# Attention written out as straight code, with a later transposition of the maxima and the sums behind the products with V

## What is computed

```
scores = einsum('bhqd,bhkd->bhqk', q, k) / sqrt(32)      # 16 heads of 32
scores = where(causal, -inf, scores)                     # self attention only
attn   = softmax(scores, axis=-1)
out    = einsum('bhqk,bhkd->bhqd', attn, v)
```

## Time and profile before

| | us |
|---|---|
| median of 3 runs | 4899.39 (4897.51 to 4901.42) |
| the profiled execution | 4905.71 |
| its span | 4904.1 |

### The profile page before, as it was taken

How to read it: one execution, slowest core, us unless ns; L and a number is a source line. 1 busy time by engine, 2 the same in 40 slices (tenths; PEclk the granted TensorE clock), 3 DMA queues, 4 the chain that set the end, 5 groups by cost and what they waited for, 6 DMA issues and landing times. The chain is left out here.

```text
span 4904.1 us, 74698 instructions
## 1 busy us (share of the span) xinstructions
PE 4388.1 (89%) x23024; PEld 2724.6 (56%) x23024; DVE 3038.8 (62%) x5530; ACT 2192.0 (45%) x4027; POOL 2321.7 (47%) x790
## 2 busy tenths in 40 slices
PE   7988999997889979999999999999996649898998
PEld 5864555546668854444444444444443427686776
DVE  4436776753633347777777777777772546676776
ACT  1213555551221105666656565556563115544554
POOL 0012333330000017888988888888894123433445
PEclk8987999998889978999999999999998869999999
DMA  4554443406455560222322222222202552322232
GB/s 143 183 164 104 105 106 89 91 16 233 169 178 175 176 159 4 53 58 58 67 53 63 53 63 57 55 53 55 53 6 99 195 181 89 97 95 92 94 108 99
DMA packets 328345, 488.99 MB, mean 100 GB/s; under 512 B 22440, under 2 KB 188328, under 8 KB 321832
## 3 DMA queue, kind: packets, MB, share of 16 engines
q1 hardware_dynamic: 318472, 468.01, 34.3%
q10 hardware_dynamic: 7232, 8.40, 0.6%
q0 software_dynamic: 2304, 8.39, 0.5%
HBM read 315.91 MB, written 168.82 MB: 99 GB/s over the span
## 5 line engine op out<-in xcount | busy, mean ns | idle before, releaser
L851 DVE TENSOR_REDUCE cross_neg_max<-cross_scores 128x1 f32<-128x512 f32 x2048 | 1261.8, 678 | 493.8 <-PE cross_scores L681 493.8
L642 POOL TENSOR_TENSOR cross_partial<-cross_partial,cross_probs 128x2048 f32<-128x2048 f32 x320 | 1464.2, 4576 | 60.6 <-ACT cross_probs L803 35.3
L803 ACT ACTIVATE cross_probs<-cross_shifted 128x512 f32<-128x512 f32 x2048 | 1105.5, 600 | 831.1 <-PE cross_shifted L693 811.0
L681 PE MATMUL cross_scores<-cross_k_stack,cross_q_stack 96*128 96x512 f32 x2048 | 880.4, 442 | 61.7 <-DMA cross_v<-v 32.7
L693 PE MATMUL cross_shifted<-cross_q_stack,cross_k_stack 98*128 98x512 f32 x2048 | 848.9, 421 | 21.3 <-issue 17.6
L693 PEld LDWEIGHTS cross_shifted<-cross_q_stack,cross_k_stack 98*128 98x128 f32 x2048 | 386.5, 190 | 392.6 <-issue 254.6
L681 PEld LDWEIGHTS cross_scores<-cross_k_stack,cross_q_stack 96*128 96x128 f32 x2048 | 397.2, 194 | 328.7 <-DVE cross_neg_max L851 251.0
L803 ACT ACTIVATE self_probs<-self_shifted 128x512 f32<-128x512 f32 (+3 forms) x768 | 359.5, 492 | 385.1 <-PE self_shifted L696 311.1
L851 DVE TENSOR_REDUCE self_neg_max<-self_scores 128x1 f32<-128x512 f32 (+3 forms) x768 | 386.1, 547 | 222.5 <-PE self_scores L684 181.9
L707 PE MATMUL cross_out<-cross_probs,cross_v 128*32 128x512 f32 x4096 | 515.8, 623 | 0.0
L1407 POOL TENSOR_TENSOR experts_v<-experts_u,experts_rows 128x512 f32<-128x512 f32 x128 | 165.2, 1290 | 478.3 <-ACT experts_u L1490 478.3
(11 more groups left out here) (208 smaller groups left out, 6666.7 us busy)
## 6 DMA issues: line engine op xcount, KB each, us to landing
cross_k_stack<-k_hi SPq DMA_DIRECT2D x32, 1024.0 KB, 19.7
experts_yt_hi<-y_hi SPq DMA_DIRECT2D x64, 512.0 KB, 3.9
experts_yt_lo<-y_lo SPq DMA_DIRECT2D x64, 512.0 KB, 4.9
self_q_stack<-q_hi SPq DMA_DIRECT2D x32, 512.0 KB, 7.0
self_k_stack<-k_hi SPq DMA_DIRECT2D x32, 512.0 KB, 14.6
out_a_in<-attn SPq DMA_DIRECT2D x16, 1024.0 KB, 9.7
x<-out_y SPq DMA_DIRECT2D x16, 1024.0 KB, 5.5
kv_x_in<-in_ctx SPq DMA_DIRECT2D x16, 1024.0 KB, 5.8
```

Source lines behind the costliest of these rows:

```text
L642: nc.gpsimd.tensor_tensor(total, total, own, ALU.add).then_inc(pool_added.sem, 1)
L681: mm = nc.tensor.matmul(scores[at][:, 0:width], q_st[0:96, w, h, q0:q0 + P], k_st[0:96, w, h, half * WIDE:half * WIDE + width], start=True ...
L803: nc.scalar.activation(probs[:, e % NE % PB, h, f:], shifted[n % SHIFTED][:, f:], ACT.Exp).then_inc(exped.sem, 1)
L851: nc.vector.tensor_reduce(neg_max[:, column(a), half:half + 1], scores[n % (SLOTS * ROUNDS) % AHEAD][:, 0:width], AX.X, ALU.max, negate=Tr ...
```

## The change

The edit does four things, all in `attend`.

- `passes` has no hardware loop any more: all 4 and 8 passes are written out.
- The transposition of a round's maxima moves behind the first `TURN_AT = 4` pieces of the next round. Items of the stream are now triples (number, round, piece), `neg_max` has two halves for even and odd rounds, VectorE's reduction to `neg` follows the last maximum at once, and `pieces_at` spreads the slots without an exception. `scored` and `maxed` get one count in advance. At the end of the last pass the transposition takes the first slot of what would be the next round.
- `LEAD` is 18 in the self attention (12 before) and 16 in the cross attention (as before).
- In the cross attention the blocks of sums move from odd steps to even ones, right behind the block of values, and `SUM_LAG` is 5, not 4, so that the partial sums come at step 4 instead of 3 and the reciprocals in steps 6 to 9 instead of 5 to 8. In the self attention the sums stay at odd steps.

```diff
-    TURN = NPIECE
+    TURN_AT = 4
     SLOTS = NPIECE + 1
-    LEAD = NPIECE // 4
+    LEAD = 18 if causal else 16
...
-    SUM_LAG = 2 if causal else 4
+    SUM_LAG = 2 if causal else 5
+    SUMS_AT = 1 if causal else 0
...
-        def done(m):
-            to = SLOTS * sum(weights[:m]) // sum(weights)
-            before = SLOTS * sum(weights[:max(m - 1, 0)]) // sum(weights)
-            return TURN - LEAD + 1 if before <= TURN - LEAD < to else to
-
+        done = lambda m: SLOTS * sum(weights[:m]) // sum(weights)
         return range(done(s), done(s + 1))
+
+    def slot(n):
+
+        q, at = n // SLOTS, n % SLOTS
+        if at == TURN_AT:
+            return n, q - 1, None
+        return n, q, at - (at > TURN_AT)
+
+    def turn_slot(q, more):
+
+        return (q + 1) * SLOTS + (TURN_AT if more or q + 1 < ROUNDS else 0)
...
-            one_pass(0, True, True)
-            with eng.Fori(1, PASSES - 1) as it:
-                one_pass(it, False, True)
-            one_pass(PASSES - 1, False, False)
+            for it in range(PASSES):
+                one_pass(it, it == 0, it < PASSES - 1)
...
-                for old in (e - 3, e - 2):
+                for old in (e - 2 - SUMS_AT, e - 1 - SUMS_AT):
                     if (old >= 0 or not begins) and not by_pool(old % NE):
                         sums(it, old)
...
-                        if h == 1 and e % 2:
+                        if h == 1 and e % 2 == 0:
+                            block_of_values(it, e, begins)
+                        if h == 1 and e % 2 == SUMS_AT:
                             block_of_sums(it, e, begins)
-                        elif h == 1:
-                            block_of_values(it, e, begins)
...
-            turn_step = next(s for s in range(NS) if any((LEAD + i) % SLOTS == TURN for i in pieces_at(s)))
-
-            def write_rows(it, q):
-                act.wait_ge(maxed.sem, maxed.at(it, SLOTS * q + SLOTS))
+            turn_step = next(s for s in range(NS) if SLOTS + TURN_AT - LEAD in pieces_at(s))
+
+            def write_rows(it, q, more):
+                act.wait_ge(maxed.sem, maxed.at(it, turn_slot(q, more) + 1))
...
+                if a == NPIECE - 1:
+
+                    dve.wait_ge(maxed.sem, maxed.at(it, n + 1))
+                    nc.vector.tensor_reduce(neg[:, 0:COLS], neg_max[:, q % 2], AX.X, ALU.min).then_inc(least.sem, 1)
+
+            def turn_rows(it, n, q):
+                turned = scores[n % (SLOTS * ROUNDS) % AHEAD]
                 dve.wait_ge(scored.sem, scored.at(it, n + 1))
```

More of the change, by code:

```diff
@@ L532, in attend @@
         partial = sb("partial", [P, NPARTIAL, 4, QB])
-        neg_max = sb("neg_max", [P, COLS, HALVES])
+        neg_max = sb("neg_max", [P, 2, COLS, HALVES])
         neg = sb("neg", [P, P])
@@ L569, in passes @@
         def passes(eng, one_pass):
-            one_pass(0, True, True)
-            with eng.Fori(1, PASSES - 1) as it:
-                one_pass(it, False, True)
-            one_pass(PASSES - 1, False, False)
+            for it in range(PASSES):
+                one_pass(it, it == 0, it < PASSES - 1)
         def stream(r, s, more):
             if r == -1:
-                return [n for n in range(SLOTS + LEAD)]
+                opening = [(n + 1, 0, n) for n in range(TURN_AT)]
+                return opening + [slot(n) for n in range(TURN_AT + 1, SLOTS + LEAD)]
             found = [SLOTS * (r + 1) + LEAD + i for i in pieces_at(s)]
-            return [n for n in found if more or n < SLOTS * ROUNDS]
+            if more:
+                return [slot(n) for n in found]
+            last = SLOTS * ROUNDS + TURN_AT
+            return [slot(n) for n in found if n < SLOTS * ROUNDS] + [(SLOTS * ROUNDS, ROUNDS - 1, None)] * (last in found)
         def load_heads(sp, bh, w):
@@ L627, in _ @@
             pool.wait_ge(filled.sem, 2)
-            pool.memset(neg_max[:, :, :], 3.0e38).then_inc(filled.sem, 1)
+            pool.memset(neg_max[:, :, :, :], 3.0e38).then_inc(filled.sem, 1)
             pool.wait_ge(filled.sem, 3)
@@ L662, in _, with score @@
             pv_done.give_credit(pe)
+            pe.sem_inc(scored.sem, 1)
             block_done.give_credit(pe)
             sum_done.give_credit(pe)
-            def score(it, n):
-                q, a = n // SLOTS, n % SLOTS
+            def score(it, item):
+                n, q, a = item
                 r = q % ROUNDS
                 pe.wait_ge(maxed.sem, maxed.at(it, user_before(n, SLOTS * ROUNDS, AHEAD) + 1))
-                if a == TURN:
+                if a is None:
                     pe.wait_ge(least.sem, least.at(it, q + 1))
@@ L749, in one_pass @@
                             score(it, n)
-                        if h == 1 and e % 2:
+                        if h == 1 and e % 2 == 0:
+                            block_of_values(it, e, begins)
+                        if h == 1 and e % 2 == SUMS_AT:
                             block_of_sums(it, e, begins)
-                        elif h == 1:
-                            block_of_values(it, e, begins)
                 if not more:
                     block_of_values(it, NE, False)
-                    for e in range(NE + 1, NE + SUM_LAG, 2):
+                    for e in range(NE + SUMS_AT, NE + SUM_LAG, 2):
                         block_of_sums_at_end(it, e)
             def block_of_sums_at_end(it, e):
-                if e == NE + 1:
+                if e == NE + SUMS_AT:
                     for old in (NE - 2, NE - 1):
@@ L805, in one_pass @@
                             if s == turn_step + 1:
-                                write_rows(it, r + 1)
+                                write_rows(it, r + 1, more)
                             if s == turn_step + 2:
@@ L833, in load_rows @@
                 act.dma_start(q_st[96:98, group(q) % BUFS, :, q0:q0 + COLS * P // 4].bitcast(F32), neg_dram).then_inc(rows_in.sem, 16)
-            write_rows(0, 0)
+            write_rows(0, 0, True)
             load_rows(0, 0)
@@ L841, in _, with max_piece @@
             maxed.give_credit(dve)
+            dve.sem_inc(maxed.sem, 1)
             rows_out.give_credit(dve)
-            def max_piece(it, n):
-                q, a = n // SLOTS, n % SLOTS
-                if a == TURN:
-                    turn_rows(it, n)
+            def max_piece(it, item):
+                n, q, a = item
+                if a is None:
+                    turn_rows(it, n, q)
                     return
@@ L850, in max_piece @@
                 dve.wait_ge(scored.sem, scored.at(it, n + 1))
-                nc.vector.tensor_reduce(neg_max[:, column(a), half:half + 1], scores[n % (SLOTS * ROUNDS) % AHEAD][:, 0:width], AX.X, ALU.max,
+                nc.vector.tensor_reduce(neg_max[:, q % 2, column(a), half:half + 1], scores[n % (SLOTS * ROUNDS) % AHEAD][:, 0:width], AX.X, ALU.max,
                                         negate=True).then_inc(maxed.sem, 1)
-            def turn_rows(it, n):
-                q = n // SLOTS
-                dve.wait_ge(maxed.sem, maxed.at(it, n))
-                nc.vector.tensor_reduce(neg[:, 0:COLS], neg_max[:, :, :], AX.X, ALU.min).then_inc(least.sem, 1)
+                if a == NPIECE - 1:
[3 more added lines that the diff above has]
+                turned = scores[n % (SLOTS * ROUNDS) % AHEAD]
                 dve.wait_ge(scored.sem, scored.at(it, n + 1))
                 dve.wait_ge(rows_out.sem, rows_out.at(it, 2 * q))
-                nc.vector.tensor_copy(neg_rows[0:COLS, 0], scores[n % (SLOTS * ROUNDS) % AHEAD][0:COLS, 0:P]).then_inc(rows_hi.sem, 1)
+                nc.vector.tensor_copy(neg_rows[0:COLS, 0], turned[0:COLS, 0:P]).then_inc(rows_hi.sem, 1)
                 dve.wait_ge(rows_hi.sem, rows_hi.at(it, q + 1))
-                nc.vector.tensor_tensor(neg_rows[0:COLS, 1], scores[n % (SLOTS * ROUNDS) % AHEAD][0:COLS, 0:P], neg_rows[0:COLS, 0].bitcast(F32),
+                nc.vector.tensor_tensor(neg_rows[0:COLS, 1], turned[0:COLS, 0:P], neg_rows[0:COLS, 0].bitcast(F32),
                                         ALU.subtract).then_inc(maxed.sem, 1)
```

## The result

The changed kernel takes 4816.1 us in the median (4812.7 to 4821.8, four runs) against 4899.0 us before. The ratio is 0.9831, with a 95% interval of 0.9814 to 0.9849. Forecast were 4823 us, between 4797 and 4862. Its profiled execution took 4812.7 us, 93 us less than the profiled execution of before, while the medians are 83 us apart: the profile of before was one of its slower runs and this one is its fastest. So I compare stages within the profiles and totals by the medians.

What follows compares the result with a forecast made beforehand. TensorE (PE) bounds the kernel, VectorE pacing long rows of pairs. Irregular time 46.4 less 5, rounds 24.7, round 0 1, self attention 9: together 76 off 4905.7, 4829.6 us profiled, 4823 median; range 4797 to 4862.

Steps and rivals of the forecast that it cites:

- Back jumps, 31 us and 5.7 us: Loops of both attentions: jumps are PE's own cost and go in full; five at 4.7 us or more cross, 5.7 self.
- the reason that the prediction gave against 108 ns: Loop jumps: PE's compare-and-branch row of 3541 ns decides against the skill's 108 ns, by which six jumps cost 0.65 us.
- Clock drops behind the transposition, ten times 1.5 us, 5 of them kept: Cross attention: ten drops of 1.5 us behind the old transposition's wait go; 5 us kept for drops from new short waits.
- The merge, neither gain nor loss to speak of: Cross attention, sums moved behind the values: worth nothing or a small loss, since VectorE can't run ahead during the sums.
- The rebuilt pieces: A cross round, values to values: 7.91, 6.19, 7.05, 7.00, 8.72, 6.19, 6.30, 6.79; 56.15 us against 57.5.
- The wait for the rows, 0.5 us net a round: Head of each cross round: load issued 1.92 us ahead of need; wait taken as 0.7 us, 0.2 given back.
- Nothing else at the wrap: Change of pass in the cross attention: only the back jump's cost was counted, going in full, with no other wait.
- rival D: Change of pass: jumps only hid another engine's wait, which comes back; 10 to 30 us left, 4870 to 4890; chance 0.07.
- The self attention, 9 us: Self attention: 5.7 us for the jump, 2 for late transposition and even pieces, 1.4 for the lead of 18.
- The ends: Cross attention's ends: 1 us gained in round 0; what the last two rounds gain is lost to POOL's last addition.
- 46.4 - 5 + 24.7 = 66 us: 29 cross rounds: irregular time 46.4, less 5 for new clock drops, plus 29 x (1.35 - 0.5) = 24.7 for regular rounds.

Runs made afterwards that it cites:

- The late load: Changed kernel with the cross attention's row load behind the third exponential of step 15, not the first: 4897.5 us, ratio 0.9993.

## Why the prediction was right

Step by step, with the prediction's term first:

- *Back jumps, 31 us and 5.7 us.* Right. Straight code alone takes 31.3 us out of the 29 rounds. In the self attention, 682.8 us remain in its profile where 689.4 were: 6.6 us. Only the reason that the prediction gave against 108 ns was too wide: it let the row of 3541 ns speak for all jumps that are taken, and the kernel's other loops have taken jumps of 0.21 to 0.24 us (last section). For the two loops of the attentions it holds.
- *Clock drops behind the transposition, ten times 1.5 us, 5 of them kept.* Too careful. None is left up to round 30; only round 0 has a slow start, as it had before. The new waits stay under 1 us. The late load shows that waits of 1.6 us bring them back.
- *The merge, neither gain nor loss to speak of.* Right in sign and mechanism. The rebuilt pieces agree within 0.2 us but for the sixth, and taking the merge out gives 19 us, of which the pieces explain 15. The text called it "nothing or a small loss"; worked out with the unmerged pieces, as for the later runs, its numbers say 0.57 us a round, and 0.53 to 0.6 is what it is.
- *The wait for the rows, 0.5 us net a round.* The mechanism is right and the size too high. The product starts some 2.4 us after the load's issue, where the prediction had 1.92 us between the two: 0.5 us late, where it took 0.7. But loading one exponential earlier brought back only 7.6 us over 31 rounds, 0.25 us each, and that in the kernel without the merge; that VectorE's pace takes up the rest is argued, not shown. The Trainium skill's figure (DMA: Bandwidth & Descriptors, the fixed cost), about 2.0 us, was 0.4 us below what the trace shows here; that page fits it on DMAs issued through GpSimd, and this one is issued from ScalarE's queue.
- *Nothing else at the wrap.* Wrong, and it cost 9.3 us that the sum didn't have. I had read the jump's gap as the only thing between two passes. Underneath lay waits for buffers that come back too early (`probs` after four steps instead of six); the cover was the jump itself, as the kernel with the loop put back shows. Of the 9.3 us, 2.9 come in straight code alone; the other 6.4 come only with the merged sums and the late transposition together. It is rival D in small.
- *The self attention, 9 us.* 10.4 us.
- *The ends.* Round 0 gave 2.0 us instead of 1. From the start of round 30 to the end of the stage it now takes 120.0 us instead of 117.2: 2.8 us of loss where I counted 0. Straight code alone has 117.2 there, with the merge 121.0, and the changed kernel without the merge 119.0, so the merge has a part in it. In the last round, which has no score products, the clock also drops twice, once right behind a wait of 0.8 us for the rows; no run parts this from POOL's additions.

For the 29 rounds the sum said 46.4 - 5 + 24.7 = 66 us, and 75 were measured. On one side stand 5 for the clock and, if the rows cost here what they cost in the kernel without the merge, about 8 for them; on the other side 9 for the wrap. Some 5 us more of gain, under 0.2 us a round, nothing here divides. So terms missed in opposite directions, and that the total of 76 us stands near the 83 of the medians is in part luck.

The sum was made against the profile, and there the gain is 93 us, not 76. Both attentions together give 75.3 + 10.4 + 2.0 - 2.8 = 85 of them. The other 8 lie in stages that the change doesn't touch, 4 between the two attentions and 4 behind the second; the profiles of the other kernels scatter there by as much, so they go with the execution and not with the change.

## What to carry to other kernels

Rebuild a stage from pieces between two fixed marks of the trace and ask for each which engine's pace holds it: here it foretold five of eight pieces to about a hundredth of a us, and, before the run that tried it, that merging two blocks on the busiest engine loses when the engine behind it needs the pause. When a loop is written out, look for what its jump had covered: buffer counters that restart with each pass come back too early at the wrap. A load that is moved a step later should keep about half a us of slack; here a wait of up to 0.4 us cost 0.25 us a round, and one of 1.64 us cost 81 / 31 = 2.6 us, over half of it because the clock fell behind it.

## What the runs showed of the hardware

A back jump of the cross attention's loop, over a body with 1188 matmuls, costs PE 3.2 to 3.9 us of idle time, and the one of the self attention's loop 3.6 us. No other engine spends a tenth of a us on its branch. The same kernel has further loops around the attentions, with bodies of 64 to 448 matmuls, and their jumps don't cost this. The branches of the loop with the longest of these bodies, in the kernel before (ns min/median/max, first and last start in us):

```profile
L192 PEldq COMPARE_BRANCH  x9: 76/208/238, 118.9 to 1674.4; - x9
```

Those that jump back last 0.21 to 0.24 us and leave PE no gap, and those that fall through 76 or 83 ns, as in the attentions (83 ns). So it isn't the jump as such that is dear. That the length of the body decides fits these rows, but no run here changed a body's length, and where the change lies between 448 and 1188 matmuls is open. The Trainium skill (Advanced Engine Details and Errata, Control Flow Timing) has 108 ns; the measured branches lie below it where they fall through and above it where they jump. Straight-line code of 8 passes was fed without one gap of this kind.

The clock doesn't follow the length of a wait alone. Waits of 1.4 us at every transposition brought it down to 1.2 GHz in eight of 29 rounds in straight code and in two of 29 with the sums merged. With the late load, waits of 1.5 to 1.9 us at the heads of rounds did so in 17 of 29, and there a wait of 1.46 us was followed by a drop and one of 1.80 us was not.
